# One GPT-like block stack on one core: projections and feed-forward in 32-column tiles, scores, mix and projections placed in a new order

## What is computed

```python
x = x + _layernorm(_L0_attn_ref(_layernorm(x), W0, Wkv, bkv, eta))   # a linear fast-weight scan over 2048 steps
x = x + _layernorm(_L0_ffn_ref(_layernorm(x), Wqkv, q_scale, k_scale, Wo, ln_g, ln_b, W1, b1, W2, b2))

for i in range(DEPTH):          # DEPTH = 6, 16 heads of 64, window 32
    x = attn_layer(shift_tokens(x), Wqkv[i], q_scale[i], k_scale[i], Wo[i]) + x
    x = ffn_layer(shift_tokens(x), ln_g[i], ln_b[i], W1[i], b1[i], W2[i], b2[i]) + x

# attn_layer: q, k, v = split(x @ Wqkv); q and k l2-normalised per head, scaled and rotated
# local attention: each window of 32 queries sees its own and the previous window's 64 keys
sim = jnp.einsum('bhwie,bhwje->bhwij', bq, bk2) * QK_SCALE; attn = softmax(where(mask, -max, sim))
out = jnp.einsum('bhwij,bhwje->bhwie', attn, bv2) @ Wo
# ffn_layer: layer norm, hg = xn @ W1 + b1 (2 x 341 wide), a * gelu(gate) @ W2 + b2
```

## Time and profile before

| | us |
|---|---|
| median of 3 runs (lowest, highest) | 1618.8 (1618.2, 1619.11) |
| the profiled execution's own time | 1619.38 |
| its span, first to last instruction | 1617.6 |
| PE busy | 1544.3 (95%) |
| DVE, ACT, POOL busy | 1234.8, 1232.5, 1222.1 (76% each) |
| TensorE's granted clock, mean | 0.987 |

### The profile page before, as it was taken

How to read it: one execution, slowest core, us unless ns; L and a number is a source line. 1 busy time by engine, 2 the same in 40 slices (tenths; PEclk the granted TensorE clock), 3 DMA queues, 4 the chain that set the end, 5 groups by cost and what they waited for, 6 DMA issues and landing times.

```text
span 1617.6 us, 69676 instructions
## 1 busy us (share of the span) xinstructions
PE 1544.3 (95%) x30224; PEld 907.8 (56%) x30224; DVE 1234.8 (76%) x1693; ACT 1232.5 (76%) x2368; POOL 1222.1 (76%) x1051
## 2 busy tenths in 40 slices
PE   7879999999999999999999999999999999999995
PEld 6745556555555555555556555555565565555553
DVE  5488878778778778777877778778778788787873
ACT  4347787787787787887887887887887887887871
POOL 6169888777787778778777787787787787787861
PEclk9989999999999999999999999999999999999998
DMA  5000000100000100000100000100000000000000
GB/s 193 28 2 27 10 7 5 61 7 6 22 6 7 35 29 10 18 7 9 36 28 10 9 16 10 33 31 9 9 16 9 7 5 9 7 18 9 7 12 27
DMA packets 24545, 32.60 MB, mean 20 GB/s; under 512 B 2372, under 2 KB 21424, under 8 KB 23344
## 3 DMA queue, kind: packets, MB, share of 16 engines
q1 hardware_dynamic: 24240, 28.15, 5.4%
HBM read 20.80 MB, written 1.05 MB: 14 GB/s over the span
## 4 chain that ended last, share of the span: by engine, by line
PE 75%; ACT 7%; issue 5%; DVE 3%; POOL 1%; DMA 0%; ACTq 0%; SPq 0%; POOLq 0%; DVEq 0%
PE ring L274 20%; PE psq L254 18%; PE ring L262 9%; PE ring L308 8%; PE pss L292 7%; PE ring L325 4%; PE ring L318 4%; PE pss L283 2%; DVE qb L927 2%; ACT L1126 2%; ACT sq L1096 1%; ACT uT L1126 1%; ACT pr L1100 1%; ACT kT L1107 1%; PE ring L649 1%
## 5 line engine op out<-in xcount | busy, mean ns | idle before, releaser
L254 PE MATMUL psq<-wqk,x0S 128*128 128x512 f32 x768 | 379.4, 617 | 4.0 <-issue 3.1
L274 PE MATMUL ring<-mh,x0S 128*32 128x512 f32 x3072 | 369.6, 598 | 7.4 <-ACT uT L1126 7.4
L1305 POOL TENSOR_TENSOR qa<-qa,qb 128x1024 f32<-128x1024 f32 x96 | 228.9, 2384 | 63.0 <-DVE qb L848 62.9
L1361 POOL TENSOR_TENSOR pr<-pr,rden 128x1024 f32<-128x1024 f32 x96 | 183.9, 1915 | 88.3 <-DVE rden L824 88.0
L1357 POOL TENSOR_TENSOR qa<-qa,qb 128x1024 f32<-128x1024 f32 x96 | 226.7, 2361 | 0.4 <-DVE qb L927 0.3
L254 PEld LDWEIGHTS psq<-wqk,x0S 128*128 128x128 f32 x768 | 135.8, 192 | 130.0 <-issue 120.8
L308 PEld LDWEIGHTS ring<-u,pT 128*32 128x32 f32 x6144 | 172.9, 111 | 61.4 <-issue 61.4
L904 DVE TENSOR_TENSOR qa<-psq,tab 128x1024 f32<-128x1024 f32 x96 | 117.5, 1224 | 105.5 <-PE psq L254 105.5
L308 PE MATMUL ring<-u,pT 128*32 128x128 f32 x6144 | 187.0, 274 | 3.2 <-ACT pT L1228 3.2
L1323 POOL TENSOR_TENSOR qa<-qa,rn 128x1024 f32<-128x1024 f32 x96 | 182.7, 1903 | 7.5
L274 PEld LDWEIGHTS ring<-mh,x0S 128*32 128x32 f32 x3072 | 80.0, 109 | 190.5 <-issue 172.6
(11 more groups left out here) (174 smaller groups left out, 2819.8 us busy)
## 6 DMA issues: line engine op xcount, KB each, us to landing
wqk<-in_wqk SPq DMA_DIRECT2D x6, 1024.0 KB, 4.9
mvT<-in_mvT SPq DMA_DIRECT2D x6, 512.0 KB, 5.6
wo<-in_wo SPq DMA_DIRECT2D x6, 512.0 KB, 8.7
xf<-x SPq DMA_DIRECT2D x24, 128.0 KB
xf<-x SPq DMA_DIRECT2D x24, 127.0 KB
rope<-in_rope SPq DMA_DIRECT2D x1, 2048.0 KB, 10.0
w<-in_w SPq DMA_DIRECT2D x6, 341.0 KB, 3.8
xmid<-in_x SPq DMA_DIRECT2D x4, 256.0 KB, 4.0
```

The source lines that it names most:

```text
L254: return mm(psq[:, 512 * (n % 2):512 * (n % 2) + 512], x0S[:, tile * P:tile * P + P], wqk[:, l % 2, 512 * n:512 * n + 512], start=True, st ...
L274: last = mm(bank[WIN * g:WIN * g + WIN, :], x0S[:, tile * P + WIN * w:tile * P + WIN * w + WIN], mh[:, l % 2, g, :, :].rearrange("p j n -> ...
L1305: g_.tensor_tensor(qa[:, t % 2, 0:1024], qa[:, t % 2, 0:1024], qb[:, 0:1024], ALU.add).then_inc(sum_q, 1)
L1361: g_.tensor_tensor(p4[t % 2], p4[t % 2], rden[:, :].unsqueeze(1).unsqueeze(3).broadcast_to([P, 2, HEADS, WIN]), ALU.mult).then_inc(p_ready, 1)
```

## The change

**In TensorE's helpers.** `project`, `hidden` and `narrow` write their result in tiles of 32 columns of weights, one matmul for each 32 PSUM partitions. `scores` and `mix` can be called by halves.

```diff
+WHOLE_P = []
+WHOLE_H = []
             def project(t, n):
 
                 tile, l = t % TILES, t // TILES
-                return mm(psq[:, 512 * (n % 2):512 * (n % 2) + 512], x0S[:, tile * P:tile * P + P],
-                          wqk[:, l % 2, 512 * n:512 * n + 512], start=True, stop=True)
+                if n in WHOLE_P:
...
+                for w in range(NWIN):
+                    last = mm(psq[WIN * w:WIN * w + WIN, 512 * (n % 2):512 * (n % 2) + 512],
+                              x0S[:, tile * P + WIN * w:tile * P + WIN * w + WIN],
+                              wqk[:, l % 2, 512 * n:512 * n + 512], start=True, stop=True)
+                return last
-            def scores(t):
+            def scores(t, half):
 
-                for pair in range(PAIRS):
+                for pair in range(4 * half, 4 * half + 4):
-            def mix(bank, t):
+            def mix(bank, t, part):
 
-                for b in range(4):
+                for b in (2 * part, 2 * part + 1):
             def hidden(bank, k, gate):
...
-                return mm(bank[0:n, :], w1[:, col:col + n], xnT[:, :], start=True, stop=True)
+                if (k, gate) in WHOLE_H:
+                    return mm(bank[0:n, :], w1[:, col:col + n], xnT[:, :], start=True, stop=True)
+                for c in range(0, n, WIN):
+                    m = min(WIN, n - c)
+                    last = mm(bank[c:c + m, :], w1[:, col + c:col + c + m], xnT[:, :], start=True, stop=True)
+                return last
             def narrow(bank):
...
-                        last = mm(bank[:, k * P:k * P + P], uT[0:n, j, k * P:k * P + P], w2[0:n, j, :],
-                                  start=(j == 0), stop=(j == 2))
+                        for w in range(NWIN):
+                            rows = slice(WIN * w, WIN * w + WIN)
+                            last = mm(bank[rows, k * P:k * P + P], uT[0:n, j, k * P + WIN * w:k * P + WIN * w + WIN],
+                                      w2[0:n, j, :], start=(j == 0), stop=(j == 2))
                 return last
```

```diff
-            for s in range(STEPS + 17):
...
+            for s in range(STEPS + 19):
...
+                t = s - 4
+                if 0 <= t < STEPS:
+                    scores(t, 1).then_inc(s_ready, 1)
...
+                    mix(ring[bank], t, 0)
...
+                t = s - 5
+                if 0 <= t < STEPS:
+                    banks = [take("P0", t), take("P1", t)]
...
+                    turn_p([ring[bank] for bank, n in banks], t)
...
+                t = s - 3
+                if 0 <= t < STEPS:
+                    wait(pe, p_shifted, t)
+                    mask(t)
...
+                    scores(t, 0)
```

More of the change, by code:

```diff
@@ L525, in _ @@
[L525 to L534, removed]
+                u = unit_at(s, 3)
+                if u >= 0:
+                    features(u)
@@ new lines, in _ @@
+                i = group_at(s, 14)
+                if i >= 0:
+                    bank, n = take("G0", i)
+                    nbank, m = place["F", i]
+                    pe.wait_ge(freed[nbank], m + 1)
+                    if i % GROUPS == 0:
+                        pe.wait_ge(w1_ready, 16 * (i // GROUPS + 1))
+                    wait(pe, freed[bank], n)
+                    hidden(ring[bank], 0, 1).then_inc(filled[bank], 1)
+                    bank, n = take("A0", i)
+                    wait(pe, freed[bank], n)
+                    hidden(ring[bank], 0, 0).then_inc(filled[bank], 1)
@@ new lines, in _ @@
+                i = group_at(s, 15)
+                if i >= 0:
+                    bank, n = take("A1", i)
+                    wait(pe, freed[bank], n)
+                    hidden(ring[bank], 1, 0).then_inc(filled[bank], 1)
+                    bank, n = take("A2", i)
+                    wait(pe, freed[bank], n)
+                    hidden(ring[bank], 2, 0).then_inc(filled[bank], 1)
+                t = s - 5
+                if 0 <= t < STEPS:
+                    bank, n = take("U1", t)
+                    wait(pe, freed[bank], n)
+                    values(ring[bank], t, 1).then_inc(filled[bank], 1)
@@ new lines, in _ @@
+                i = group_at(s, 14)
+                if i >= 0:
+                    bank, n = place["A1", i]
+                    dve.wait_ge(filled[bank], n + 1)
+                    gbank, m = place["G1", i]
+                    dve.wait_ge(freed[gbank], m + 1)
+                    rows = HBLK[1][1]
+                    v.scalar_tensor_tensor(uT[0:rows, 1, :], ring[bank][0:rows, :], par[0:rows, i // GROUPS, 3:4],
+                                           uT[0:rows, 1, :], ALU.add, ALU.mult).then_inc(freed[bank], 1)
@@ L1202, in _ @@
[L1202 to L1210 removed]
+                i = group_at(s, 11)
@@ new lines, in _ @@
+                if i >= 0:
+                    act.wait_ge(nmr_ready, i + 1)
+                    if i > 0:
+                        abank, m = place["A2", i - 1]
+                        act.wait_ge(filled[abank], m + 1)
+                    for k in range(QUAD):
+                        last = nc.scalar.activation(xh[:, k * P:k * P + P].rearrange("p (a n) -> p a n", a=2), xf[:, :, k, :],
+                                                    ACT.Identity, bias=nmr[:, k:k + 1], scale=rstd[:, k:k + 1])
+                    last.then_inc(xh_ready, 1)
```

691 lines of the change are left out of this document (322 added, 369 removed).

## The result

The changed kernel takes **1577.6 us** (median of four runs, 1576.9 to 1578.0) where the kernel before took 1619.0 beside it (1618.2 to 1619.3): a ratio of 0.9745, with a 95% interval of 0.9728 to 0.9762. Its profiled execution has a span of 1576.2 us, 41.4 shorter than before.

A forecast was written before the change was run, and what follows sets the result against it. The prediction took TensorE's own groups, including changes of tile form, to bound the kernel. Terms -31 - 2 - 5 - 5 - 7 + 0 + 8 = -42 took 1619.4 us to 1577 us, range 1554 to 1611.

The forecast's parts named there:

- Part 1: TensorE's order: fewer changes of tile form and fewer entries into whole-array work, -31 us, bounds 19 us either way.
- Part 2: Project, hidden and narrow in tiles: 512-column calls cost the same as whole, narrow gets cheaper, -2 us.
- Part 3: Scores and mix in halves: scores start on queued instructions, -5 us; halving mix costs nothing.
- the second half follows the slow turns and may profit: Step behind the -5 us for halved scores; the first half directly follows the mask as before.
- both halves under 0.75: Sign set for the new timeline: each scores half takes under 0.75 us including its exit.
- Part 4: TensorE's instruction stalls around mask, scores and P turn: -5 us of the 9, bounds -9 and +9.
- fetch: Rival: a 1.71 us instruction stall in every fourth step, none of the old ones gone, 1623 us; chance 0.04.
- Part 5: ScalarE's gelus grouped ahead of Exp: fewer table loads, U1's wait for the gelu gone, -7 us, bounds -7 and 0.
- Part 7: New waits in the psq loop between project k and q: +8 us, bounds 0 and +30; covered by about 0.5 us.
- light loop: Rival: the psq loop costs 0.25 us more a step than taken, giving 1601 us; chance 0.17.
- Part 6: Filling and draining with two more tiles in flight: 0 us, bounds -8 and +8.
- what the extra tiles lack at the start they leave as work at the end: Step behind the 0 us for filling and draining: the two extra tiles' work moves from start to end.

The follow-up runs named there:

- e1: The changed kernel with the four project calls whole-array again, everything else as changed: 1623.0 us, ratio 1.0019.
- e2: The changed kernel with hidden and narrow whole-array again: 1601.9 us, ratio 0.9893.
- e3: The kernel before, its order untouched, with project, hidden and narrow in 32-column tiles: 1615.6 us, ratio 0.9973.
- e4: The changed kernel with scores half 1 moved behind half 0, both at the end of the step: 1637.0 us, ratio 1.0104.
- e7: The changed kernel with mask and both scores halves moved directly behind the k and q turns: 1656.2 us, ratio 1.0218.
- e9: The changed kernel with mask and both scores halves behind the two turns, and project, hidden and narrow whole-array again: 1703.4 us, ratio 1.0529.
- e5: The changed kernel with ScalarE's gelu of G2 moved behind Exp, so tables swap four times a group instead of twice: 1647.0 us, ratio 1.0158.
- e10: The changed kernel with a 256-column VectorE memset (0.27 us) added before k's first multiply in every tile: 1579.9 us, ratio 0.9765.
- e11: The changed kernel with a 768-column VectorE memset (698 ns) added before k's first multiply in every tile: 1619.8 us, ratio 1.0003.

## Why the prediction was right, and where it was right by luck

The total was forecast at -42 us and measured at -41. The terms did not all come out so; three errors cancelled, and in that the total was luck. In the middle of the span, where 19 of 24 groups lie, I scale by 24/19.

- **Part 1, changes of form (forecast -31): confirmed.** e1 and e2 put 45 and 24 us back (38 and 28 by the same count). Exits cost 0.11 to 0.12, entry into the whole array 0.08 to 0.10, as the rows of before had it. The changes that before never made cost the same: the P turn still takes 0.64 with the mask behind it, and a half of scores 0.79 with mix behind it. With that my bounds of 19 us either way were far too wide. The count holds for the tiles alone too (e3: 19 us by the starts, 20 forecast); what it cannot see is that the old order gives most of it back as waits.
- **Part 2, the calls in tiles (forecast -2): confirmed.** A pair is 1.72 in a run, 0.86 a call, narrow 2.75 with its exit (824.97 to 827.72). The Trainium skill's figure ("TensorE: Matmul & The Clock Gate", Part 3), by which three column tiles together take 1.26 times one, would have made 1695; 0.86 us for a call in four tiles, the same as whole, disagrees.
- **Part 3, halves (forecast -5): wrong in sign.** Both halves take 0.79 + 0.77 = 1.56 against 1.40 in one piece; one more exit of 0.10 was in part 1, so 0.06 a step are left, +6 us. The two turns side by side gave 0.04 a step of it back (1.14 instead of 1.18). The failed step is "the second half follows the slow turns and may profit". What the split is good for I had not named: it keeps the burst short and stands as a cover between the turns and mix (59 us more without it, e4). The sign that I had set, both halves under 0.75, did not come.
- **Part 4, instruction stalls (forecast -5): right in sign, too small.** 12 us of "issue" stalls in the layers fell to 3, so -9, at the end of my bound; 2.6 us of new ones came in the fill. (The longest burst of the new order is the two turns with half 1, 192 instructions, not the 176 that I counted.) e7 and e9 show that I weighed the mechanism much too lightly: 168 short matmuls in a row cost 55 to 59 us in stalls alone. The rival *fetch* had a real mechanism and 0.04 of chance; that the new order avoids it was the point to argue.
  The Trainium skill's sentence ("Runtime: NRT & Kernel Launch", Instruction fetch mechanics) that the fetch is mostly hidden fits after, with 2.9 us in the layers, and not e7. That these stalls are instruction fetch no row says in words, but their times do: PE goes on 2.2 to 2.8 us behind a packet of the instruction queue (e7, e9).
- **Part 5, ScalarE's tables (forecast -7): confirmed.** The wait is gone, 7.4 us. In the new order more hangs on it: with G2's gelu behind Exp it would have been not 7 us but 69 (e5), for its place and the tables together.
- **Part 7, new waits (forecast +8): did not come.** The multiply of k does wait for T1 of t - 2 (DVE idle 57.8 us in 40 times for the turns of L264 in after, and 75.0 us in 33 for GpSimd's tables), but PE has no wait for either square between the first and last X. The loop is covered on both sides, but on the side of k by about 0.2 us only (e10, e11), less than half of what I computed for the shortest step. So the rival *light loop* was near: a square of k that comes 0.5 us later in those steps would have cost 0.3 in each of them.
- **Part 6, filling and draining (forecast 0): wrong, about +10.** The ends hold five groups' work, which at the rate of the middle (40.8 / 19 = 2.1 us a group) should have gained 11 us; they gained 0.6. The failed step is "what the extra tiles lack at the start they leave as work at the end" taken as free. I tested no cause. The trace shows two things that the fill has more of than before. Project waits 10.4 us for the squares there, where it waited 0.7. And TensorE is slow for longer: the mean granted clock is 0.67 between 80 and 120 us and 0.91 between 120 and 160 (before 0.79 and 0.96), and six project pairs run there at 3.0 to 3.6 us instead of four. I had looked at the fill for its chain alone, and not for its waits and its clock.

The sum by what was measured: PE's busy time in the middle -26.8 x 24/19 = -34 (parts 1 to 3 forecast -38; of the -34 the halves are +6, the two turns side by side -4, and -36 are left for parts 1 and 2, forecast -33); its idle time there -14.0 x 24/19 = -18 (parts 4, 5 and 7 forecast -4); the ends +10 (forecast 0). That is -42. The forms brought about what was forecast, the halves cost where I had a gain, the waits gave 14 us more than forecast, and the ends lost ten.

**What stays open.** Of e4's 59 us some 12 have no row, of e7's 79 some 20. In e3 it is open what holds PE up in the stalls without a bracket. What the ends lost, and what e5 owes to the tables alone, was not tested. No version in this study beat the changed kernel.

## What to carry to other kernels

Count the changes of form in the order as it will be, with both neighbours of each call: a form change costs 0.1 us on each side of a whole-array call and 0.1 behind a tile call, so tiles and order belong together: tiles pay most where equal forms stand next to each other, and an order pays only once the forms are equal. Then look at what the waits take back; the tiles alone saved 19 us of PE's own work here and kept 4. Before an order is judged by its sum, look at what each piece covers: pieces of 0.8 us and a single activation carried 59 and 69 us here, by waits that no row of the kernel before or after shows. Where a forecast rests on "covered by half a microsecond", pad that side on purpose with two sizes; the two times and the starts give the slack itself.

## What was unexpected of the hardware

- 168 short matmuls in a row (turns, mask, scores) stall PE by 1 us on average, 60 times in 96 steps, with no engine to wait for (e7: 59 us in 60 stalls, e9: 55 in 52). PE goes on 2.2 to 2.8 us behind a packet of the instruction queue, in 57 of 59 and in 50 of 52. Before and e4, with 152 in a row, have 12 and 18 us; after, with 96 at one place (turns, half 1) and 88 at another (P turn, mask, half 0), has 2.9.
- Behind a wait of PE of 2.5 us the granted clock was 0.50 for the next 2.6 us, though TensorE had been at full clock before (e5). It fell so behind ten of 22 such waits of 1.8 to 2.6 us and not behind the other twelve. On average a wait cost 1.3 times its length (69 us for 52.8).
- A matmul of 512 columns costs 0.86 us whole and in four column tiles alike, with four times the instructions.
